# Pair 1 of a routed low-rank layer in seven products in place of eight (Trainium2, one core)

## The reference, cut to what matters

```python
def _L0_cond_ref(x, condition, weights):        # per batch of 64 rows a 64x64 matrix out of 16
    W = weights[condition]
    return jnp.einsum('bct,bcd->bdt', x, W)

def _L0_ffn_ref(x, W_base, b_base, W_gate, A, B):
    result = jnp.einsum('bnd,od->bno', x, W_base) + b_base
    logits = jnp.einsum('bnd,ed->bne', x, W_gate)
    probs = jax.nn.softmax(logits, axis=-1)
    top_p, top_i = jax.lax.top_k(probs, 2)
    top_p = top_p / jnp.sum(top_p, axis=-1, keepdims=True)
    route_w = jnp.sum(one_hot(top_i, 8) * top_p[..., None], axis=-2)
    h = jnp.einsum('bnd,erd->bner', x, A)       # 8 experts of rank 16
    hw = h * route_w[..., None]
    delta = jnp.einsum('bner,eor->bno', hw, B)
    return result + delta
x = x + _L0_ffn_ref(_L0_cond_ref(x, ...), ...)  # x: 128 batches x 64 rows x 1024
```

## Time and profile before

| | before |
|---|---|
| median of 3 runs | 939.77 us (939.57 to 940.12) |
| the profiled execution | 939.31 us, span 937.5 us, so 1.81 us lie outside the span |
| granted TensorE clock over the span | 1.00 |
| busy: PE, DVE, ACT, POOL | 99%, 70%, 40%, 55% |

### The profile page before, as it was taken

One profiled execution on the slowest core, in us unless ns is written; L12 is line 12 of the kernel. 1 busy time (PEld: TensorE's weight loads), 2 busy tenths in 40 slices (PEclk: granted clock), 3 DMA queues, 4 the chain that ended last, 5 costly groups with the idle time before them and its releaser, 6 DMA issues.

```text
span 937.5 us, 17674 instructions
## 1 busy us (share of the span) xinstructions
PE 932.6 (99%) x5415; PEld 880.5 (94%) x5415; DVE 660.8 (70%) x2272; ACT 379.7 (40%) x810; POOL 516.0 (55%) x506
## 2 busy tenths in 40 slices
PE   9999999999999999999999999999999999999998
PEld 7999999999999999999999999999999999999997
DVE  5787667676677676676766777667767667676675
ACT  5553343443434434434334344343443443433432
POOL 3566555654556545566555565455664555655550
PEclk9999999999999999999999999999999999999999
DMA  9523333323333233232333332332323423223312
GB/s 306 189 79 108 128 112 112 106 84 123 117 107 123 77 113 134 91 132 89 101 123 112 112 108 82 123 125 99 123 86 104 134 100 124 95 95 123 112 68 90
DMA packets 41452, 107.13 MB, mean 114 GB/s; under 512 B 4449, under 2 KB 8674, under 8 KB 41442
## 3 DMA queue, kind: packets, MB, share of 16 engines
q1 hardware_dynamic: 41440, 107.01, 33.7%
q10 hardware_dynamic: 2, 0.00, 0.0%
HBM read 73.43 MB, written 33.55 MB: 114 GB/s over the span
## 4 chain that ended last, share of the span: by engine, by line
PE 99%; DMA 1%; SPq 0%; ACT 0%; DVE 0%; issue 0%; DVEq 0%
PE ps L832 54%; PE ps_r L832 19%; PE ps_out L850 11%; PE ps_out L860 9%; PE ps L891 3%; DMA w_sum<-in_w_t 1%; PE ps L902 1%; PE ps_r L891 1%; PE ps L877 0%; PE ps_r L877 0%; PE ps L850 0%; PE ps L860 0%; ACT w_hi L434 0%; SPq L239 0%; SPq L233 0%; PE ps_hwt L856 0%
## 5 line engine op out<-in xcount | busy, mean ns | idle before, releaser
L320 POOL TENSOR_TENSOR a_lo<-raw,a_hi 128x512 fp32r<-128x512 f32 x128 | 168.5, 1327 | 153.8 <-ACT a_hi L422 152.1
L651 DVE STREAM_TRANSPOSE ps_hwt<-hw 32x32 f32<-32x32 f32 x944 | 210.4, 223 | 29.5
L832 PE MATMUL ps<-w_hi,s_hi 128*128 128x448 f32 x480 | 176.0, 367 | 0.0
L832 PE MATMUL ps<-w_lo,s_hi 128*128 128x448 f32 x480 | 174.2, 363 | 0.0
L832 PE MATMUL ps<-w_hi,s_lo 128*128 128x448 f32 x480 | 173.8, 362 | 0.0
L832 PE MATMUL ps_r<-r_lo,a_hi 128*128 128x264 f32 x496 | 141.3, 285 | 0.0
L832 PE MATMUL ps_r<-r_hi,a_hi 128*128 128x264 f32 x496 | 140.8, 284 | 0.0
L832 PE MATMUL ps_r<-r_hi,a_lo 128*128 128x264 f32 x496 | 140.8, 284 | 0.0
L832 PE MATMUL ps<-w_hi,a_hi 128*128 128x448 f32 x360 | 131.4, 365 | 0.0
L832 PE MATMUL ps<-w_hi,a_lo 128*128 128x448 f32 x360 | 131.1, 364 | 0.0
L832 PE MATMUL ps<-w_lo,a_hi 128*128 128x448 f32 x360 | 130.7, 363 | 0.0
(11 more groups left out here) (135 smaller groups left out, 1698.2 us busy)
## 6 DMA issues: line engine op xcount, KB each, us to landing
raw<-in_x_t SPq DMA_DIRECT2D x128, 256.0 KB, 2.7
o_sb<-in_x SPq DMA_DIRECT2D x64, 512.0 KB, 4.0
out_x<-o_sb SPq DMA_DIRECT2D x62, 512.0 KB, 2.6
w_sum<-in_w_t SPq DMA_DIRECT2D x8, 448.0 KB, 9.5
r_raw<-in_w_t SPq DMA_DIRECT2D x4, 264.0 KB, 5.5
table_raw<-in_cond_w SPq DMA_DIRECT2D x2, 256.0 KB, 9.1
b_raw<-in_b_t SPq DMA_DIRECT2D x1, 512.0 KB, 10.9
out_x<-o_sb SPq DMA_DIRECT2D x2, 224.0 KB, 2.1
```

Source lines behind the costliest of these rows:

```text
L320: pool.tensor_tensor(a_lo[j][:], raw[j][:], as_f32(a_hi[j][:]), ALU.subtract).then_inc(s_a_lo[j], 1)
L651: dve.transpose(ps_hwt[c * TURN:(c + 1) * TURN, r * TURN:(r + 1) * TURN], hw[r * TURN:(r + 1) * TURN, c * TURN:(c + 1) * TURN]).then_inc(s ...
L832: mm = pe.matmul(bank[:, 0:w.shape[-1]], a[:, k, :], w[:, k, :], start=(opens and k == 0 and q == 0), stop=(closes and k == KH - 1 and q = ...
```

## The change

Pair 1 is done with seven products as well. The places that the rest of the text speaks of:

- **PE**, `first()`: P1, P2 and the four halves of R come first, then P3, P6, P5, P7, P4. P3 takes S4 from `a_hi`, `a_lo` of A12.
- **DVE**: T1 is summed in two halves, in the routing steps of pair 0. T3, T2, NT4 follow, and the additions of `step` are now in `first()` too.
- **POOL**: the sums S1 to S4 of pair 1 and their four rests. The sums of pair 2 now wait for products of pair 1.
- **ACT**: tops of S1 to S4 of pair 1, and a copy of P1.
- **SP**: loads of pair 2 into `raw` wait for the sums (A11) and for S4's rest (A12). In the loop, semaphore counts are raised by one; nothing else changes.

```diff
             # POOL
+            sum_s1(1, True)
             a_rest(1, A11)
+            sum_s2(1, True)
+            sum_s3(1, True)
             a_rest(1, A12)
-            a_rest(1, A21)
-            a_rest(1, A22)
+            sum_s4(1)
 
             def first():
+                s_rest(1, 1, s1[:], s1_hi, s1_lo)
+                a_rest(1, A21)
+                a_rest(1, A22)
                 pool.wait_ge(s_mixed[0][Q], 1)
                 fetch_mix(1, 0)
                 pool.wait_ge(s_mixed[1][R], 1)
                 fetch_mix(1, 1)
-                sum_s3(2, True)
-                sum_s1(2, True)
+                s_rest(1, 2, s2[:], s2_hi, s2_lo)
+                s_rest(1, 3, s3[:], s3_hi, s3_lo)
+                s_rest(1, 4, raw[A12][:], a_hi[A12], a_lo[A12])
                 a_rest(2, A11)
                 a_rest(2, A12)
-                sum_s2(2, True)
+                sum_s1(2)
+                sum_s2(2)
                 sum_s4(2)
+                sum_s3(2)
...
             # DVE, pair 0
             rank_experts(0, 0)
+            dve.wait_ge(s_w0_lo["B11"], 2)
+            dve.wait_ge(s_w0_lo["B12"], 2)
+            t_sum(1, T1, T3, T1, ks(0))
+            weigh_experts(0, 0)
...
             rank_experts(0, 1)
+            t_sum(1, T1, T3, T1, ks(1))
             weigh_experts(0, 1)
-            dve.wait_ge(s_w0_lo["B11"], 2)
-            t_sum(1, T1, T3, T1)
...
             # PE
             def first():
                 pe.wait_ge(s_a_lo[A11], 2)
-                first_q(ps_1, 0, 0, "B11").then_inc(s_p[1], 1)
+                strassen(ps_1, a_hi[A11], a_lo[A11], B11, True).then_inc(s_p[1], 1)
                 mix_chunk(0, 1, Q)
                 mix_chunk(0, 1, R)
+                turn_hw(1)
+                pe.wait_ge(s_p1_out, 1)
                 pe.wait_ge(s_a_lo[A12], 2)
-                first_q(ps_1, 0, 1, "B21").then_inc(s_p[2], 1)
...
+                strassen(ps_1, a_hi[A12], a_lo[A12], B21, False).then_inc(s_p[2], 1)
                 pe.wait_ge(s_hwt_lo, 2)
                 for c in (L, Q, R):
                     lora(1, c)
...
                 plain_r(ps_r, 0, 0, True, False)
                 plain_r(ps_r, 0, 1, False, True).then_inc(s_r_sum[0], 1)
...
+                plain_r(ps_5, 1, 0, True, False)
+                mix_chunk(1, 0, L)
                 pe.wait_ge(s_a_lo[A22], 2)
...
+                plain_r(ps_5, 1, 1, False, True).then_inc(s_r_sum[1], 1)
+                pe.wait_ge(s_s_lo[4], 1)
+                strassen(ps_1, a_hi[A12], a_lo[A12], B22, True).then_inc(s_p[3], 1)
+                pe.wait_ge(s_s_lo[2], 1)
+                pe.wait_ge(s_t_lo[2], 1)
+                strassen(ps_6, s2_hi, s2_lo, T2, True, lambda: turn_hw(2)).then_inc(s_p[6], 1)
+                pe.wait_ge(s_s_lo[1], 1)
+                pe.wait_ge(s_t_lo[1], 1)
+                pe.wait_ge(s_z_lo[1][R], 2)
+                strassen(ps_5, s1_hi, s1_lo, T1, True).then_inc(s_p[5], 1)
+                pe.wait_ge(s_s_lo[3], 1)
+                pe.wait_ge(s_t_lo[3], 1)
+                pe.wait_ge(s_u2, 1)
+                strassen(ps_6, s3_hi, s3_lo, T3, False).then_inc(s_p[7], 1)
                 mix_chunk(1, 0, R)
...
+                pe.wait_ge(s_t_lo[4], 1)
+                pe.wait_ge(s_u3, 1)
+                strassen(ps_6, a_hi[A22], a_lo[A22], NT4, False).then_inc(s_p[4], 1)
+                mix_chunk(1, 0, Q)
+                lora(0, Q)
```

More of the change, by code:

```diff
@@ L165, in adaln_ffn @@
         s_p1_out = sem("P1_copied")
+        s_p3_in = sem("pair1_P3_added")
         s_u2 = sem("P1_P6_added")
@@ L276, in step @@
                     sp.wait_ge(s_a_lo[A11], 2)
-                elif not last:
-                    sp.wait_ge(s_s_sum[2], p - 1)
                 if not last:
+                    sp.wait_ge(s_s_sum[2], p)
+                    sp.wait_ge(s_s_sum[3], p)
                     load_raw(p + 1, A11)
@@ L288, in step @@
                 load_x(p, 0)
[L289 to L292, removed]
                 if not last:
+                    sp.wait_ge(s_s_lo[4], p)
                     load_raw(p + 1, A12)
@@ L333, in sum_s2 @@
             def sum_s2(p, early=False):
-                pool.wait_ge(s_s_sum[1], p - 1)
+                pool.wait_ge(s_s_sum[1], p)
                 if not early:
@@ L347, in sum_s4 @@
             def sum_s4(p):
-                pool.wait_ge(s_s_sum[2], p - 1)
+                pool.wait_ge(s_s_sum[2], p)
                 pool.wait_ge(s_a_lo[A12], p + 1)
@@ L390, in first @@
                 fetch_mix(1, 1)
-                sum_s3(2, True)
-                sum_s1(2, True)
+                s_rest(1, 2, s2[:], s2_hi, s2_lo)
+                s_rest(1, 3, s3[:], s3_hi, s3_lo)
+                s_rest(1, 4, raw[A12][:], a_hi[A12], a_lo[A12])
                 a_rest(2, A11)
                 a_rest(2, A12)
-                sum_s2(2, True)
+                sum_s1(2)
+                sum_s2(2)
                 sum_s4(2)
+                sum_s3(2)
+                s_rest(2, 2, s2[:], s2_hi, s2_lo)
                 s_rest(2, 3, s3[:], s3_hi, s3_lo)
-                s_rest(2, 2, s2[:], s2_hi, s2_lo)
                 s_rest(2, 1, s1[:], s1_hi, s1_lo)
@@ L443, in added_top, with p1_out @@
             def added_top(p, t, c, whole=None):
-                act.wait_ge(s_z_sum[t, c], p - 1)
+                act.wait_ge(s_z_sum[t, c], p)
                 z_top(t, c, whole if whole is not None else added[t, c])
+            def p1_out(p):
+                act.wait_ge(s_p[1], p + 1)
+                act.wait_ge(s_mixed[1][L], p)
+                act.copy(z_sum[1][:, cols(L)], ps_1[:, 0:NS]).then_inc(s_p1_out, 1)
             def seed(p, t, c, first=False):
@@ L500, in _ @@
             a_top(1, A11)
+            sum_top(1, 1, s1[:], s1_hi)
             pe_hwt_top(1)
@@ L515, in first @@
             def first():
+                p1_out(1)
+                pe_hwt_top(2)
+                t_top(1, T1)
+                sum_top(1, 2, s2[:], s2_hi)
                 act.wait_ge(s_p[2], 2)
                 z_top(0, L, ps_1[:, 0:NS])
-                pe_hwt_top(2)
-                t_top(1, T1)
+                sum_top(1, 3, s3[:], s3_hi)
+                t_top(2, T2)
                 seed(1, 0, L)
+                act.wait_ge(s_r_sum[0], 2)
+                sum_top(1, 4, raw[A12][:], a_hi[A12])
@@ L521, in first @@
+                seed(1, 0, R)
                 seed(1, 0, Q)
-                seed(1, 0, R)
-                act.wait_ge(s_p[7], 2)
-                t_top(2, T2)
+                z_top(0, R, ps_r[:, 0:width[R]])
+                t_top(4, NT4)
+                act.wait_ge(s_r_sum[1], 2)
+                z_top(1, R, ps_5[:, 0:width[R]])
                 exps(2)
+                t_top(3, T3)
+                pe_hwt_top(3)
+                a_top(2, A11)
                 act.wait_ge(s_p[3], 2)
-                z_top(0, Q, ps_6[:, 0:NS])
@@ L528, in first @@
[L528 to L533, removed]
-                a_top(2, A12)
-                act.wait_ge(s_p[5], 2)
-                z_top(1, Q, ps_5[:, 0:NS])
+                a_top(2, A12)
+                a_top(2, A21)
+                sum_top(2, 2, s2[:], s2_hi)
+                added_top(1, 0, Q, ps_r[:, 0:NS])
+                seed(1, 1, L)
@@ L537, in first @@
+                added_top(1, 1, Q)
                 sum_top(2, 3, s3[:], s3_hi)
-                sum_top(2, 2, s2[:], s2_hi)
+                added_top(1, 1, L)
+                seed(1, 1, R)
                 sum_top(2, 1, s1[:], s1_hi)
-                seed(1, 1, L)
                 act.wait_ge(s_p[4], 2)
-                z_top(1, L, ps_1[:, 0:NS])
-                seed(1, 1, R)
+                a_top(2, A22)
                 seed(1, 1, Q)
-                act.wait_ge(s_r_sum[1], 2)
-                z_top(1, R, ps_r[:, 0:width[R]])
@@ L547, in first @@
-                a_top(2, A21)
-                a_top(2, A22)
             def step(p, last):
-                act.wait_ge(s_p[1], p + 1)
-                act.wait_ge(s_mixed[1][L], p)
-                act.copy(z_sum[1][:, cols(L)], ps_1[:, 0:NS]).then_inc(s_p1_out, 1)
+                p1_out(p)
                 exps(2 * p - 1)
@@ L621, in w_target, with t_sum @@
                 return w_hi[:, T2] if lo is None else w_lo[:, lo]
-            def t_sum(t, to, one_at, other_at):
-                dve.tensor_tensor(w_sum[:, to], w_sum[:, one_at], w_sum[:, other_at],
+            def t_sum(t, to, one_at, other_at, part=slice(0, KH)):
+                dve.tensor_tensor(w_sum[:, to, part, :], w_sum[:, one_at, part, :], w_sum[:, other_at, part, :],
                                   ALU.subtract).then_inc(s_t_sum[t], 1)
@@ L727, in _ @@
             rank_experts(0, 1)
+            t_sum(1, T1, T3, T1, ks(1))
             weigh_experts(0, 1)
-            dve.wait_ge(s_w0_lo["B11"], 2)
-            t_sum(1, T1, T3, T1)
             def first():
-                z_rest(1, 0, L, ps_1[:, 0:NS])
+                dve.wait_ge(s_t_sum[1], 2)
+                t_sum(3, T3, T2, T3)
```

(67 more changed lines are left out.)

14 lines of the change are left out of this document (4 added, 10 removed).

## The result

| | before | after |
|---|---|---|
| median | 939.94 us (6 runs) | 948.18 us (6 runs) |
| ratio | | 1.0088, 95% interval 1.0077 to 1.0099 |
| the profiled execution | 939.31 us | 948.02 us, span 946.3 us |

The change makes the kernel slower by 8.2 us, 0.9%. The forecast was 947.4 us, with a range of 942 to 949.5.

What follows compares the result with a forecast made beforehand. PE, busy 99% of the span, was taken as the bound. Saving 2.43 us against waits of 6.2, 1.5 and 0.6 and 1.8 for the clock gave +7.7 us: 947.0 for the profiled execution, median 947.4, range 942 to 949.5.

Steps and rivals of the forecast that it cites:

- What PE saves: Pair 1 on PE: one product of eight, 12 matmuls at 0.2025 us, is taken out, saving 2.43 us.
- The stall ahead of P3: Pair 1: PE waits for S4's rest on POOL, 6.2 us, with bounds from 4.4 to 0.3 more.
- the turns of 1.88 and 1.16: Ahead of P3: DVE operations with two SBUF inputs and POOL operations alternate, 1.88 + 1.16 = 3.04 us a turn.
- The layout: Hand-made timeline up to P3: PE wants S4's rest at 49.1, POOL ends it at 55.5.
- The later waits: Behind P3: PE stalls 1.5 us for z and 0.6 us for tile 1's L; bounds 0 and 2.4.
- The clock: After PE's idle stretch ahead of P3 the clock falls to its lower level, costing 1.8 us; bounds 0 and twice 1.8.
- the clock staying up: Rival: the same waits, but PE's clock does not fall, so without 1.8: 945.6 us; chance 0.30.
- Priced at nothing or 0 to 0.3: Pair 1: ACT's five more operations and SP's loads hidden; P1's copy 0.2 if uncovered, pair 0's tile 1 routing 0 to 0.3.
- Sum: All terms: -2.43 + 6.2 + 1.5 + 0.6 + 1.8 = +7.7 us, forecast median 947.4 us.
- POOL getting through in time: Rival: no turns with DVE arise, POOL ends at 46.9, before 49.1, PE loses nothing: 937.3 us; chance 0.11.
- Missed turns: Rival: P3 waits 2 to 3 us, the clock stays, later stalls shrink: 938 to 941.5 us; chance 0.06.

Runs made afterwards that it cites:

- e6: Changed kernel with DVE's T3, T2, NT4 and T2's rest reading their second input from PSUM, and ACT's tops of pair 2's S2, S3 moved later: 937.40 us.
- e1: Changed kernel with DVE's T3, T2, NT4 and T2's rest taking their second input from PSUM instead of SBUF (results not the T matrices): 939.54 us.
- e3: Changed kernel with S4's rest placed ahead of the rests of S2 and S3 on POOL: 942.25 us.
- e5: Changed kernel with ACT's top of pair 2's S2 placed behind the top of tile 0's Q: 947.56 us, median of four.
- e2: Changed kernel with 28 matmuls of zeros placed on PE ahead of P3, before the wait for S4's rest: 946.64 us.

## Why the prediction was right, step by step

- **What PE saves, 2.43**: e6 gives 2.45, with an interval of 1.5 to 3.2.
- **The stall ahead of P3, 6.2**: 6.25. Right in its parts too: the turns of 1.88 and 1.16, the copies that wait, and T1's rest ahead of S4's. The layout had PE ready at 49.1 and S4's rest done at 55.5; the trace has 49.98 and 56.17. Both are late by 0.7 to 0.9 alike, so the difference held and the two times did not. That is luck in part: the layout left out delays on both lists, 0.5 on POOL's by S4's sum (done at 37.62, laid out for 37.1), and PE's at two places named below, and they happened to be alike. e1 shows the cause, e3 the place in the queue.
- **The later waits, 1.5 and 0.6**: 1.49 and 0.53. e5 shows ACT's order as the cause of the first, e6 against e1 that it is the cause of both.
- **The clock, 1.8**: it fell, and cost 4.62 - 2.43 = 2.2 in the trace after the change and 1.5 in e5's. e2 shows that it was the idleness. The term was a choice between two values that no row decided (the clock staying up had a chance of 0.30), and its size was borrowed from ten other matmuls, so that 1.8 lies between the two measured values is luck in part. The windows of the trace before give those ten a granted clock of 1.00 (the last number but two):

```profile
3.00:4.00 1.00, 1.00 (x4) 0.39 (x3) 0.00 (x0) 0.42 (x1) 0.00 (x0) 1.00 1.00 313
```

That they ran at the lower level is read from their pitch alone: 0.41 us, against 6.22 / 28 = 0.22 for the same matmuls in e2. The Trainium skill ("TensorE: Matmul & The Clock Gate", The HAM clock gate) says that the array falls to 1.2 GHz when it has been idle. The trace after the change agrees: 0.50 from 56.20 to 60.85.

- **Priced at nothing or 0 to 0.3**: the largest miss. P1 of pair 1 starts at 35.59 and not at 35.43, and P2 at 39.48 and not at 38.84:

```profile
35.59 0.37 PE L860 MATMUL ps<-w_hi,a_hi 128*128 128x448 f32 x1
...
39.38 0.33 PE L884 MATMUL ps_hwt<-ident,hw 128*128 128x128 f32 x1 [0.23 <-DVE hw L703]
39.48 0.44 PE L860 MATMUL ps<-w_hi,a_hi 128*128 128x448 f32 x1
```

So the move of b_lo and T1's halves into the routing cost about 0.6 together. I had named the second as 0 to 0.3; its half of T1 stood behind S4's sum and made the routing end at 39.32 and not 38.8. I had not priced DVE's b_lo on PE's path at all: with the half of T1 ahead of it (1.83, stretched by POOL's S1 sum) hwt_rest behind it came late by 0.2. No run moved these two alone.

- **Sum**: -2.43 + 6.25 + 2.02 + 2.19 + 0.6 = 8.6, against 8.71 between the profiled executions. The forecast had 7.7: of the 1.0 that it lacked, 0.6 is the term priced at nothing and 0.4 the clock.

The rivals: POOL getting through in time is what e1 brings about, at 939.5. The price of 937.3 named for it left out the later waits, which don't hang on the turns ahead of P3; only e6, with ACT's order changed too, comes to 937.4. Missed turns, at 2 us of wait, is e3; where the clock stayed up it took 941.7 to 942.3, above the 938 to 941.5 named for it, since the later waits did not shrink as the rival had assumed.

Still open is why the same wait ahead of P3 costs 1.5 us of clock in one execution and 2.2 in another, and whether the wait of 2.0 in e3 is what lowers the clock in three of its seven executions.

## What to carry to other kernels

Where DVE works on two SBUF inputs and POOL works at the same time, add up POOL's list and these operations of DVE as if one engine had them, and see what the sum does to the operation that the busiest engine waits for; the engines' separate shares (70% and 56% here) hide it. Then put first in each queue what is wanted first: moving one line was worth 5.9 us, more than twice the whole saving at stake. A wait of PE costs more than its length if it is long enough to lower the clock, so first bring down the longest.

## What the runs showed of the hardware that was not expected

- DVE's `tensor_tensor` of 1792 elements takes 2.01 us with the second input in PSUM, read by a broadcast over four blocks (e1), and 2.02 to 2.05 with both in SBUF. Moving the second input to PSUM costs nothing by itself here, and frees POOL.
- After one and the same wait of 6.25 us P3 took 4.62 us in one execution and 3.97 in another (e5), and with a wait of 2.0 us three of seven executions had a mean clock of 0.998 and four of 1.00 (e3). A term for the clock is better given as a range than as one value.
